# A fused audio block on one core: expert weights split ahead of the first scatter, the first expert product moved, and VectorE for the low parts of the last stage

## The reference

```python
logits = xf @ router_w                      # 8 experts
probs = softmax(logits)
topw, topi = top_k(probs, 2)
h = silu(einsum('nd,edf->nef', xf, w1))
ye = einsum('nef,efd->ned', h, w2)
routed = einsum('ne,ned->nd', combine, ye)
gate, up = split(xf @ shared_gate_up)
shared = silu(gate) * up @ shared_down
out = h_in + routed + sigmoid(xf @ shared_gate_w) * shared
```

## Time and profile before

| | |
|---|---|
| runs | 1127.31, 1123.14, 1126.66 us; median 1126.66 |
| profiled execution | 1124.56 us, of which the span of the instructions is 1122.8 us |
| PE busy | 1054.9 us (94% of the span) |
| DVE busy | 767.5 us (68%) |
| ACT busy | 670.2 us (60%) |
| POOL busy | 523.2 us (47%) |
| mean granted clock of PE | 0.985 of full speed |
| chain that ended last | PE 70%, DVE 9%, POOL 6%, issue 5%, ACT 2% |

### The profile page before, as it was taken

One profiled execution on the slowest core, in us unless ns is written; L12 is line 12 of the kernel. 1 busy time (PEld: TensorE's weight loads), 2 busy tenths in 40 slices (PEclk: granted clock), 3 DMA queues, 4 the chain that ended last, 5 costly groups with the idle time before them and its releaser, 6 DMA issues.

```text
span 1122.8 us, 23554 instructions
## 1 busy us (share of the span) xinstructions
PE 1054.9 (94%) x8042; PEld 882.3 (79%) x8042; DVE 767.5 (68%) x1975; ACT 670.2 (60%) x2059; POOL 523.2 (47%) x565
## 2 busy tenths in 40 slices
PE   6979999999999999999999999999998968899996
PEld 5867788878777887877788787878767868799985
DVE  3756766785777578577857867775774765466678
ACT  4647775774777477577747757774773534455541
POOL 0024543545546354654635464463444447544432
PEclk9989999999999999999999999999999999899998
DMA  8110000001000000100000010000022723344476
GB/s 262 58 44 1 2 1 20 2 3 38 20 1 30 30 1 1 39 20 1 30 22 9 1 40 20 2 30 16 15 68 84 236 75 112 102 141 134 125 303 212
DMA packets 46442, 65.93 MB, mean 59 GB/s; under 512 B 7960, under 2 KB 39448, under 8 KB 45304
## 3 DMA queue, kind: packets, MB, share of 16 engines
q1 hardware_dynamic: 39576, 46.60, 13.1%
q0 software_dynamic: 6480, 17.83, 4.3%
q10 hardware_dynamic: 272, 0.00, 0.0%
HBM read 36.09 MB, written 28.33 MB: 57 GB/s over the span
## 4 chain that ended last, share of the span: by engine, by line
PE 70%; DVE 9%; POOL 6%; issue 5%; ACT 2%; another core or an unknown queue 1%; DMA 1%; SPq 0%; DVEq 0%; ACTq 0%; POOLq 0%
PE pT_ps L710 10%; PE o_ps L723 9%; PE proj_ps L69 9%; PE proj_ps L71 9%; PE proj_ps L70 8%; PE s_ps L696 8%; POOL prob L1639 3%; PE v_ps L69 2%; POOL prob L1641 2%; PE v_ps L70 2%; PE v_ps L71 2%; PE s_ps L69 2%; PE s_ps L71 2%; PE s_ps L70 2%; PE pT_ps L955 2%
## 5 line engine op out<-in xcount | busy, mean ns | idle before, releaser
L1010 ACT ACTIVATE prob<-s_ps,nmax 128x255 f32<-128x255 f32 x512 | 239.0, 478 | 227.8 <-DVE nmax L1213 227.6
L1639 POOL TENSOR_SCALAR prob<-prob,rinv 128x255 f32<-128x255 f32 x128 | 139.7, 1091 | 373.5 <-DVE rinv L1231 370.6
L1213 DVE TENSOR_REDUCE nmax<-s_ps 128x2 f32<-128x510 f32 x256 | 166.3, 682 | 37.7 <-PE s_ps L696 36.2
L710 PEld LDWEIGHTS pT_ps<-ident,prob 128*128 128x128 f32 x1024 | 109.6, 141 | 60.8 <-issue 49.8
L710 PE MATMUL pT_ps<-ident,prob 128*128 128x128 f32 x1024 | 146.0, 281 | 6.7 <-POOL prob L1641 3.5
L1238 DVE COPY probT<-pT_ps 128x512 f32<-128x512 f32 x128 | 88.5, 691 | 77.0 <-PE pT_ps L710 77.0
L723 PE MATMUL o_ps<-probT,v 128*64 128x256 f32 x1024 | 139.6, 394 | 1.2 <-DVE oT_lo L1244 1.2
L696 PE MATMUL s_ps<-qk_space 64*128 64x256 f32 x1536 | 125.5, 296 | 5.3 <-ACT prob L1010 4.6
L1641 POOL TENSOR_SCALAR prob<-prob,rinv 128x255 f32<-128x255 f32 x128 | 119.2, 931 | 0.0
L696 PEld LDWEIGHTS s_ps<-qk_space 64*128 64x128 f32 x1536 | 99.2, 186 | 21.9 <-issue 8.7
L1010 ACT ACTIVATION_READ_ACCUMULATOR prob<-s_ps,nmax 128x1 f32 x512 | 106.3, 208 | 0.0
(11 more groups left out here) (268 smaller groups left out, 2739.4 us busy)
## 6 DMA issues: line engine op xcount, KB each, us to landing
xg<-expert_in_rows SPq DMA_DIRECT2D x71, 130.0 KB
back<-expert_out_rows SPq DMA_DIRECT2D x8, 1024.0 KB, 13.2
xin<-in_x_dram SPq DMA_DIRECT2D x8, 512.0 KB, 4.5
z_rows<-z SPq DMA_DIRECT2D x8, 512.0 KB, 3.2
z<-z_rows SPq DMA_DIRECT2D x8, 512.0 KB, 5.7
expert_in_rows<-bo_row SPq DMA_DIRECT2D x16, 128.0 KB
raw_up<-in_L_ffn_w_dram SPq DMA_DIRECT2D x8, 256.0 KB, 5.1
raw_down<-in_L_ffn_w_dram SPq DMA_DIRECT2D x8, 256.0 KB, 6.1
```

Of the source, the lines that this page charges most:

```text
L710: m = pe.transpose(pT_ps[h][:, o:o + P], prob[u_par(i)][:, h, qt, kt * P:(kt + 1) * P], ident[:])
L1010: m = act.activation(prob[u_par(i)][:, h, qt, 1:N], s_ps[h][:, qt * N + 1:(qt + 1) * N], ACT.Exp, bias=nmax[u_par(i)][:, n:n + 1], accum_o ...
L1213: dve.tensor_reduce(nmax[u_par(i)][:, 2 * h:2 * h + 2], s_ps[h][:].rearrange("p (q k) -> p q k", q=2)[:, :, 1:N], AX_X, ALU.max, negate=Tr ...
L1639: pool.tensor_scalar(prob[k][:, 0, 1, 1:N], prob[k][:, 0, 1, 1:N], rinv[k][:, 1:2], None, ALU.mult).then_inc(s_nA1, 1)
```

## The change

- The weights of all eight experts are split ahead of the first scatter. ACT makes the high parts of experts 4 to 7 too, between the copies of groups 2 and 3; POOL makes all low parts: that of expert 0 ahead of its wait for `s_table`, that of expert 1 between the low parts of groups 2 and 3, and those of experts 2 to 7 behind them. `split_both` is gone.
- POOL instead of DVE makes the low parts of the hidden columns of groups 2 and 3.
- `up(0)` stands ahead of `shared_rows(3)` on PE, and `add_shared(3)` behind `x_lo(1)` on DVE.
- On DVE `product(2, 1)` stands ahead of `z3_lo(3)`, and the first two reductions of `tile_words` are a function of their own.
- `transpose_z3(4)` and `z3_lo(4)` move into the last step of the expert loop.
- In the last stage DVE instead of POOL makes the low parts, and the order of adds and products on DVE is another. `EXPERTS_FIRST` is 7, so that group 6 adds the shared rows first.

```diff
-        EXPERTS_FIRST = 6
+        EXPERTS_FIRST = 7
...
@@ PE @@
                 hidden(g, 1)
                 shared_rows(g - 1)
-            shared_rows(SHARED_EARLY - 1)
...
             up(0, e[0])
+            shared_rows(SHARED_EARLY - 1)
             for n in range(RUN):
...
+                if n == RUN - 1:
+                    transpose_z3(SHARED_EARLY)
                 if n + 1 < RUN:
                     up(n + 1, e[n + 1])
...
-            transpose_z3(SHARED_EARLY)
             down_rows(RUN - 1, e[RUN - 1])
@@ ACT @@
             silu(2, 0)
+            split_hi(2)
             z3_hi(3)
             hidden_split_hi(2, 0)
             silu(2, 1)
+            split_hi(3)
             hidden_split_hi(2, 1)
-            split_hi(2)
+            split_hi(4)
+            split_hi(5)
             silu(3, 0)
-            split_hi(3)
+            split_hi(6)
             hidden_split_hi(3, 0)
             silu(3, 1)
+            split_hi(7)
             hidden_split_hi(3, 1)
@@ DVE @@
-            hidden_split_lo(1)
+            hidden_split_lo(1, 0)
+            hidden_split_lo(1, 1)
             turns_past()
             add_shared(0)
             product(2, 0)
+            product(2, 1)
             z3_lo(3)
+            tile_sums()
             tile_words()
-            product(2, 1)
-            hidden_split_lo(2)
             add_shared(1)
             product(3, 0)
             product(3, 1)
-            hidden_split_lo(3)
             add_shared(2)
-            add_shared(3)
...
             x_lo(1)
+            add_shared(3)
             for n in range(RUN):
...
                     y_copy(n - 1)
+                if n == RUN - 1:
+                    z3_lo(SHARED_EARLY)
...
-            z3_lo(4)
             product(4, 0)
             z3_lo(5)
+            hidden_split_lo(4, 0)
             product(4, 1)
+            hidden_split_lo(4, 1)
+            product(5, 0)
             add_experts(0)
-            product(5, 0)
+            hidden_split_lo(5, 0)
             z3_lo(6)
+            product(5, 1)
+            hidden_split_lo(5, 1)
             add_experts(1)
-            product(5, 1)
-            add_experts(2)
+            add_shared(4)
             product(6, 0)
             z3_lo(7)
-            add_shared(4)
+            hidden_split_lo(6, 0)
+            product(6, 1)
+            add_experts(2)
+            hidden_split_lo(6, 1)
+            add_shared(5)
+            product(7, 0)
             add_experts(3)
-            product(6, 1)
+            hidden_split_lo(7, 0)
+            product(7, 1)
+            hidden_split_lo(7, 1)
             add_experts(4)
-            product(7, 0)
-            add_shared(5)
+            add_shared(6)
             add_experts(5)
-            product(7, 1)
             add_experts(6)
-            add_shared(6)
@@ POOL @@
+            split_lo(0)
             pool.wait_ge(s_table, TABLE_STEPS)
-            for e in range(HI_BY_SCALAR):
+            hidden_split_lo(2)
+            split_lo(1)
+            hidden_split_lo(3)
+            for e in range(2, E):
                 split_lo(e)
...
-            split_behind = {3: 4, 7: 5, 11: 6, 17: 7}
             for n in range(RUN):
                 scatter(n)
-                if n in split_behind:
-                    split_both(split_behind[n])
-
-            for g in range(SHARED_EARLY, GROUPS):
-                hidden_split_lo(g)
```

More of the change, by code:

```diff
@@ L354, in main_phase @@
     BUFS = 6
-    HI_BY_SCALAR = 4
+    RAW_FIRST = 4
     HEAD = 16
@@ L516, in main_phase @@
         s_raw = [sem(f"expert{e}_in") for e in range(E)]
-        s_w_hi, s_w, s_half = sem("expert_hi"), sem("expert_split"), sem("expert_hi_by_pool")
+        s_w_hi, s_w = sem("expert_hi"), sem("expert_split")
         s_x_in = [sem(f"xg{k}_in") for k in range(BUFS)]
@@ L621, in _ @@
             sp.wait_ge(s_wo, 2 * GROUPS)
-            for e in range(HI_BY_SCALAR):
+            for e in range(RAW_FIRST):
                 load_expert(e)
@@ L626, in _ @@
             load_z3(3)
-            for e in range(HI_BY_SCALAR, E):
+            for e in range(RAW_FIRST, E):
                 load_expert(e)
@@ L1373, in turns_past, with tile_sums, tile_words @@
                 done(dve.tensor_tensor(past_rows, past, skips[0:1].unsqueeze(2).broadcast_to(shape), ALU.mult))
-            def tile_words():
+            def tile_sums():
                 dve.tensor_reduce(table_e, past.rearrange("a e t -> a t e"), AX_X, ALU.add)
                 done(dve.tensor_reduce(table_r, past_rows.rearrange("a e t -> a t e"), AX_X, ALU.add))
+            def tile_words():
                 dve.tensor_scalar(table_e, table_e, float(E - 1), None, ALU.min)
@@ L1403, in z3_lo, with hidden_split_lo @@
                                       ALU.subtract).then_inc(s_zl3, 1)
[L1405 to L1409, removed]
+            def hidden_split_lo(g, c):
+                dve.wait_ge(s_hhi, FC * g + c + 1)
+                dve.tensor_tensor(h_lo[g % 2][:, c, :], h_full[:, c, :], f32(h_hi[g % 2][:, c, :]),
+                                  ALU.subtract).then_inc(s_hlo, 1)
             def product(g, c):
@@ L1702, in split_lo @@
                 m.then_inc(s_w, 1)
[L1704 to L1712, removed]
             router_step(GROUPS, 1)
```

## The result

The changed kernel takes 1115.43 us (median of 5 runs, 1113.78 to 1116.56), the kernel before 1126.66 in the same comparison. The ratio is 0.9902 with a 95% interval of 0.9881 to 0.9922: 11.2 us faster, against 1115.5 forecast. The profiled execution took 1116.56.

The account below looks back on a forecast made before the run. It took PE's waits to bound the kernel, with DVE setting the end: 3.8 + 7.0 + 0.8 - 1.4 = 10.2 us gained. This gives 1114.4 from the profiled execution, 1116.5 from the median; middle 1115.5, range 1109 to 1123.5.

Parts of the forecast that it names:

- The loop: Expert loop: removing four packs (scatters back to back on POOL) gains 10.7 us, one new pack costs 3.7; net 7.0.
- 10.7: Steps 9 to 26: 12.9 us of excess less 2.2, charged to some 20 packed scatters at 0.53 us each.
- Rival (2): Loop keeps its pace; early stalls come from instruction fetching or loads of x; gain 3.2, 1122.5 us, chance 0.22.
- the rule: Trainium skill's SBUF page: a DMA never contends with a compute engine, so packs could not hold ACT; supports rival (2).
- the new pack: Start of the loop: after POOL's splits end at 924.8, scatters catch up in one pack of 7, costing 3.7 us.
- the 4.1 us by which scatter 0 was to be late: Start of the loop: scatter 0, due at 920.7, waits for POOL's splits until 924.8, making a pack of 7 scatters.
- The head: Ahead of the expert loop: transposes of h of step 0 start at 915.5 instead of 919.26; gain 3.8 us (3.1 to 4.5).
- Seam and last stage: Loop's end: earlier transposes of group 4 gain 0.8 us; last stage: DVE's added low parts and gaps lose 1.4 (0 to 3).
- the walk through DVE's queue: Last stage: DVE's instructions timed one by one from PE's start, 38.9 us work and 7.6 gaps, ending at 46.4 or 46.5.
- Rival (3): Last stage: incoming `back` loads, not POOL, slow DVE's long adds; gain 5.3 us, so 1120.5, chance 0.1.
- (4): All is gained and the long pack costs nothing, or first stalls vanish too: 13.9 us and up, 1109 to 1112, chance 0.12.
- (5): POOL's twelve subtractions take the contended 1.71 us, its splits end at 933.7, a longer pack follows: 1130 us, chance 0.06.

Follow-up runs that it names:

- experiments 1 and 2: 1: changed kernel, POOL holding scatters 20, 28, 36, 44 so packs form, 1125.74 us; 2: kernel before, splits cut into pieces behind scatters 1 to 24, 1115.49 us.
- 8: Changed kernel, low parts of experts 4 to 7 in halves behind scatters 0 to 15, table read and `shared_rows(3)` ahead of x's transposes: 1112.13 us.
- experiment 6: Changed kernel with seven instead of six buffers for expert tiles, so each load of x is issued one step earlier: 1110.35 us, ratio 0.9871.

## Why the forecast was right, step by step

**The loop (7.0 forecast, 5.9 and 6.0 measured).** The steps 9 to 26 gave 11.0 and 10.2 where 10.7 was charged to the packs, and experiments 1 and 2 show the cause from both sides. Rival (2), the loop keeping its pace, falls on the two slower chips, and with it what the rule would have made of the time.

The sum of 10.7 was right and the count under it was not. The prediction speaks of four to five scatters in a pack and some 20 in all; the trace of the kernel before has packs of 4, 3, 4 and 4 (935.83 to 939.68, 944.61 to 947.20, 954.34 to 958.21, 970.15 to 974.00), 15 in all. That is 0.7 us each, not 0.53. As the four packs went away whole, the count dropped out.

It did not drop out of the new pack, which was to have 7 scatters and cost 3.7. It held 4, and cost 3.4 and 1.9 in the two traces, and 18.5 - 16.8 = 1.7 in the mean of the eight traces with it against the three without (before, 2 and 8). The term that failed is the 4.1 us by which scatter 0 was to be late. Its result was ready at 920.9, and results usually wait 0.8, so it was due at 921.7 and left at 924.1: 2.4 us late, since the head had gained less and POOL ended 0.9 us sooner. At 0.6 us a scatter, which the first two kept to, 2.4 us are 4 scatters. And steps 26 to 70, forecast unchanged, became 1.7 and 2.3 us longer. Most of that lies in steps 26 to 52, whose stalls experiment 6 puts down to loads of x; why these are a little later than before is not settled.

**The head (3.8 forecast, 2.1 and 2.2 measured).** `hidden(3, 0)` came 1.6 us later than before, or 2.4 when the 0.8 us that the attention had gained are set aside, as forecast (2.2). The step that failed is from x(0) on. The forecast let PE go from the transposes to `up(0)` in 1.9 us; it took 2.7, since x(1) landed 0.55 us late. And it took the middle between full and low clock for the shared rows. The low clock came in full, and on `up(0)` as well: 912.75 to 916.49 for the rows instead of 2.9, and 1.44 instead of 0.72 for `up(0)`. That is 0.8 + 0.8 + 0.7 = 2.3 against the 0.7 that 915.5 had in it: 1.6 us, about what is missing. The lower bound of 3.1 us had the low clock in full, 1.4 us against the 0.8 + 0.7 measured; what puts the gain below it is the 0.8 us in front of `up(0)`.

**Seam and last stage.** 0.7 for 0.8, and a loss of 1.5 for 1.4, with the stage at 46.6 us where the walk through DVE's queue had given 46.4 to 46.5. The split between the two is less sure than it looks: by experiment 4 the new order alone costs 0.6, and the 0.7 gained at the seam does not reach the end of the old order. Rival (3) falls: the adds took 1.22 beside the same loads. Rivals (4) and (5) fall too: the new pack costs something, and POOL ended its splits at 923.9 with 1.26 to 1.30 us each, not 1.71.

**The sum.** By the two traces the gain in span is 8.0 and 8.7 us, by the medians 11.2 (8.8 to 13.4 by the interval of the ratio). Against the 8.0 the forecast of 10.2 is too high by the head (1.7) and the loop (1.1), while 0.8 us came ahead of all changed code and is no work of the change. And the median of before stood 2.1 us above its profiled execution while that of after stands 1.1 below. So part of the agreement at 1115.5 is owed to those two, not to the working.

## What to carry to other kernels

Look at the spacing of indirect transfers on POOL, not only at POOL's busy time, and measure on more than one chip: on one of three here the packs cost nothing. If an engine that issues them has other work, cut it into pieces and put one between each two, rather than a block after which the transfers catch up back to back. And before filling a gap of PE with a reordering, look at the granted clock behind it: short transposes between waits can cost the following matmuls more than the gap saved.

## What was not expected of the hardware

- Three or four scatters 1.27 us apart delay what ACT and DVE get from PE by about 2 us, on the two slower chips of three. The price comes to 0.4 to 0.7 us a packed scatter. What carries it (SBUF, the path of semaphores, the queues of DMA) is open; the trace calls it "remote". A seventh x buffer leaves it as it is, so it isn't a late load.
- One chip of three shows none of it, with eight scatters in a row both ahead of the loop and in it, and runs the kernel before in 1113.56 us instead of 1126. A kernel's gain may thus be a gain on some chips alone.
- PE's clock was at 1.2 GHz for 3.4 us behind two single pairs of transposes between waits of 0.69, 0.55 and 1.27 us. Behind one wait of 1.11 us with full work on both sides it was at 2.4 GHz, and fell only behind the next two waits, of 1.13 and 0.47 us.
